# Narrow attention: maxima turned earlier, first head groups loaded in the projection, and an unread F32 product beside each early row pair

## The chip, the cores and the metric

The kernel runs on one core of a Trainium2 chip. The metric is device microseconds (us) of one execution. Before the change three runs gave 2531.52, 2533.64 and 2536.02 us; their median, 2533.64 us, is the time before. The engines are named as in the profile: PE is TensorE (PEld its weight loads), DVE VectorE, ACT ScalarE, POOL GpSimd, SP SyncE, which here only issues DMAs.

## The reference

The input `x` is 4 x 512 x 256 in F32. Four blocks follow one another, each `x = x + layernorm(block(layernorm(x)))`:

```
A  causal attention, 16 heads of 16: softmax(q k^T / 4, causal) v, then W_out + bias
B  mixture of 32 experts, 6 a token, squared relu, plus a shared expert
C  attention, 16 heads of 16 (q1|q2, k1|k2 of 8 each), no mask:
   softmax(q1 k1^T * s - lam * q2 k2^T * s) v, then W_proj
D  grouped attention (16 heads of 128, 4 key heads) and a mixture of 8 experts, 2 a token
```

The change touches stages A and C only: the projection that makes q, k and v, and the attention behind it.

## The kernel before

Stages A and C call the same three functions: `narrow_projection` (L160), `narrow_attention` (L590) and `narrow_output` (L954). Each is a block of its own with a barrier behind it.

The projection works through four groups of 512 tokens (one batch each). A group is normalized, transposed on PE, copied to `hT` by ACT, multiplied by the weights (8 products of 128x512 for q and k, 8 of 128x256 for v), and q and k are split into a high part in FP32R (ACT, L302) and a low part (DVE, L268). SP stores both parts to the DRAM tensors `q_parts` and `k_parts` with four DMAs of 512 KB (L209), waits until the group's stores have landed (L210) and only then lets ACT write the parts of the next group (`parts_free`, L211). POOL fills the spare rows of the attention's tiles `qs` and `ks` meanwhile: zeros for q, ones for k (L280, L281).

The attention works in quads of four heads: 4 quads a batch, 16 in a stage. A quad's q and k lie in SBUF as two slots of two heads; a head has rows 0 to 47 for three partial products of the high and low parts, and rows 48 and 49 of q for the negated row maximum (high and low), against ones in k. There are four buffers `qs[0..3]`, `ks[0..3]`. Loading a quad takes 12 DMAs of 64 KB (`load_half`, L648). For each quad PE makes the scores twice:

- `rows` (L692): scores with queries on the partitions, one pair of heads at a time, in two PSUM places; DVE takes the row maxima (L913), which frees the place. In stage A masks are added by four small products a pair (L706).
- POOL splits the maxima (L866, L868), `turn_maxima` (L723) transposes them on PE, `keep_maxima` on ACT copies them to `mT` (L812), and SP places them with four DMAs in the q tiles (`place_maxima`, L663).
- `cols` (L730): scores with keys on the partitions, now with the maximum subtracted by the extra rows; ACT takes exp (L829), POOL cuts the diagonal in stage A (L882), and `values` (L739) multiplies by v in F32 with a sum column; `turn_quad` (L752) and DVE divide.

PE's order is written out by hand: at the start the `rows` of quads 0 and 1 (L785 to L792), then in quad n, for each of the four key tiles kt, `cols` of the next tile, `rows` of quad n+2, the turn of the maxima of quad n+1 after kt = 1, the turn of quad n-1's output at kt = 2, and `values` of tile kt. Scores by key, the turned maxima and the turned output share a ring of three PSUM banks; `place`, `TM_AT` and `TQ_AT` give each its position in that ring. ACT follows the same order and copies the maxima after the exps of kt = 2.

The loads of quads 0 and 1 are issued when the attention block begins, q by SP and k by ACT; then SP issues the two loads of the mask in stage A (L674, L675) and quads 2 and 3.

Of the kernel before, what the change touches and what calls it, by code (L numbers as in the profile page):

```python
# [5 lines left out]
F32 = mybir.dt.float32  # L6
# [153 lines left out]
def narrow_projection(c, name, w_qk, w_v, b_qk, b_v, lambdas, q_parts, k_parts, qs, ks, vals):  # L160
# [5 lines left out]
    with ExitStack() as ctx:  # L166
# [18 lines left out]
        stored, parts_free, constant = sem("stored"), sem("parts_free"), sem("constant")  # L185
        tr, ps, pv = c.bank[0:2], c.bank[2:6], c.bank[6:8]
# [6 lines left out]
        with block:  # L193
            @block.sync
            def _(sp):
                sp.sem_inc(parts_free, 1)
                sp.dma_start(wqk[:, :, :], weights(w_qk)).then_inc(w_in, 16)
# [7 lines left out]
                with sp.Fori(0, B) as b:  # L205
# [5 lines left out]
                    sp.sem_inc(parts_free, 1)  # L211

# [377 lines left out]
def narrow_attention(c, name, q_parts, k_parts, qs, ks, vals, out, mask):  # L590
# [19 lines left out]
    with ExitStack() as ctx:  # L610
# [17 lines left out]
        loaded = [sem(f"loaded{s}") for s in range(4)]  # L628
# [18 lines left out]

        def load_half(eng, t, src, parts, quad, s):  # L648
            for g in range(2):
                for j, part in enumerate(parts):  # L650
                    r = PAIR * g + HD * j
                    rows = src[part, bass.ds(quad, 1), :, :].rearrange("a (u g d) s -> g d (a u) s", g=2, d=HD)[g]
                    eng.dma_start(t[r:r + HD, :, :].bitcast(F32), rows).then_inc(loaded[s], 16)

        block = nc.Block()
        with block:
            @block.sync
            def _(sp):
                def load_quad(quad, s):
                    load_half(sp, qs[s], q_parts, (0, 0, 1), quad, s)  # L660
                    load_half(sp, ks[s], k_parts, (0, 1, 0), quad, s)

                def place_maxima(n, s):  # L663
                    sp.wait_ge(mT_ready, n + 1)
                    for slot in range(2):
                        for g in range(2):
# [9 lines left out]
                for s in range(2, 4):  # L676
                    load_quad(s, s)
                place_maxima(0, 0)
                with sp.Fori(0, B - 1) as b:
                    for s in range(BQ):  # L680
# [3 lines left out]
                        load_quad(n + 4, s)  # L684
                for s in range(BQ - 1):
                    place_maxima(NQUAD - BQ + s + 1, s + 1)
                for s in range(4):
                    sp.wait_ge(m_loaded[s], 64 * B)

            @block.tensor  # L690
            def _(pe):
                def rows(n, s, qt, slot, first):  # L692
# [9 lines left out]
                    if causal:  # L702
                        for i in range(2):
                            for g in range(2):
# [3 lines left out]
                                if i == 1:  # L708
                                    mm.then_inc(rows_done, 1)

# [19 lines left out]
                def cols(b, s, kt, slot):  # L730

                    lo = first_query(kt)
                    if kt == 0 and slot == 0:
                        pe.wait_ge(m_loaded[s], 64 * b + 64)
# [23 lines left out]
                def quad(b, s, ahead, following, first):  # L758
# [3 lines left out]
                    for kt in range(NQ):  # L762
                        for slot in range(2):
# [1563 lines left out]
```

## Time and profile before

| what | value |
|---|---|
| runs, median | 2533.64 us |
| profiled execution | 2537.47 us |
| its span, first to last instruction | 2535.6 us |
| busy: PE, DVE, ACT, POOL | 79%, 66%, 48%, 29% |
| mean granted PE clock | 0.854 of 2.4 GHz |
| stage A: projection, attention, output | about 12 to 81, 81 to 371, 372 to 444 us |
| stage C: projection, attention, output | about 888 to 969, 969 to 1208, 1209 to 1242 us |

The page's slices of PE's clock (tenths, 63.4 us each) begin 9 5 5 5 5 5 6 6 9: the digits from the second to the sixth are the attention of stage A, where PE is granted about half its clock. The shares of busy time above are means over stages with different limits, so they say little of one stage; the rows further on are by stage.

### The profile page before, as it was taken

Reading aid. Unit: us, or ns where it says so; the run is one execution under the profiler, and the core shown is the slowest. Engines: PE = TensorE matmul, PEld = TensorE weight load, DVE = VectorE, ACT = ScalarE, POOL = GpSimd, SP = SyncE. Lnnn points to the kernel's source line nnn. Section 1 sums busy time; section 2 is a strip of 40 time slices with the busy share of each in tenths; the row PEclk is TensorE's granted clock in tenths of the full one; section 3 lists DMA queues with packets and bytes.
Section 4 is the critical chain, followed back from the end, with each engine's and each line's share of the span. In section 5 each row is a group of like instructions: output and inputs, shape, how many; then the busy total and the mean of one; then the engine's idle time right before and its main releaser. Section 6 shows DMA issues by size and latency. Waiting matters only on the chain. (4 is left out here: it accounts for less than half of the span.)

```text
span 2535.6 us, 41622 instructions
## 1 busy us (share of the span) xinstructions
PE 2010.2 (79%) x12514; PEld 1565.1 (62%) x12514; DVE 1670.2 (66%) x3522; ACT 1222.4 (48%) x2616; POOL 729.7 (29%) x817
## 2 busy tenths in 40 slices
PE   6599986399999765887477769999979807999990
PEld 3366645299999632332355537677759707999990
DVE  5344426788888775785678767777754416888865
ACT  1144431244444312777145448888863206777750
POOL 3022222255555430000145544444430140000005
PEclk9555556699999976999789889999989758999995
DMA  3511100000000025220122223222236316555523
GB/s 122 115 52 52 51 8 1 33 17 25 25 25 17 0 92 120 59 62 25 71 83 83 99 112 109 83 108 107 83 132 213 112 66 243 207 207 213 215 106 99
DMA packets 93281, 231.54 MB, mean 91 GB/s; under 512 B 13456, under 2 KB 39184, under 8 KB 86032
## 3 DMA queue, kind: packets, MB, share of 16 engines
q1 hardware_dynamic: 88976, 220.59, 25.2%
q0 software_dynamic: 3072, 8.39, 1.0%
q10 hardware_dynamic: 1152, 1.57, 0.5%
q8 instruction: 40, 0.66, 0.1%
q14 instruction: 41, 0.34, 0.0%
HBM read 157.10 MB, written 72.88 MB: 91 GB/s over the span
## 5 line engine op out<-in xcount | busy, mean ns | idle before, releaser
L544 POOL TENSOR_SCALAR d_att_probs<-d_att_probs,d_att_rinv 128x128 f32<-128x128 f32 (+2 forms) x192 | 177.6, 925 | 219.2 <-DVE d_att_rinv L555 219.1
L1439 DVE SCALAR_TENSOR_TENSOR b_acc<-bank,b_gates,b_acc 128x256 f32<-128x256 f32 x512 | 212.4, 477 | 41.7 <-PE bank L1354 41.7
L1407 POOL TENSOR_TENSOR b_moe_act_low<-b_moe_act,b_moe_act_high 128x512 fp32r<-128x512 f32 x136 | 175.9, 1294 | 177.5 <-ACT b_moe_act_high L1384 177.5
L434 PE MATMUL wide<-d_att_k,d_att_q 128*128 128x128 f32 (+3 forms) x512 | 188.1, 450 | 18.7 <-DMA d_att_k<-k_dram 18.5
L2017 PE MATMUL wide<-e_moe_hT_high,e_moe_w_high 128*128 128x256 f32 x644 | 183.2, 284 | 14.2 <-DVE e_moe_w_low L2087 14.2
L913 DVE TENSOR_REDUCE a_att_rmax<-wide 128x2 f32<-128x256 f32 (+3 forms) x128 | 104.7, 824 | 130.2 <-PE wide L706 129.6
L913 DVE TENSOR_REDUCE c_att_rmax<-wide 128x2 f32<-128x1024 f32 x128 | 155.3, 1223 | 49.9 <-PE wide L698 45.2
L2017 PE MATMUL wide<-e_moe_hT_high,e_moe_w_low 128*128 128x256 f32 x644 | 183.0, 284 | 0.0
L2017 PE MATMUL wide<-e_moe_hT_low,e_moe_w_high 128*128 128x256 f32 x644 | 183.0, 284 | 0.0
L491 ACT ACTIVATE d_att_probs<-wide,d_att_nmax 128x128 f32<-128x128 f32 (+3 forms) x256 | 135.4, 529 | 78.8 <-DVE d_att_nmax L550 78.8
L829 ACT ACTIVATE c_att_probs<-bank 128x512 f32<-128x512 f32 x256 | 139.1, 596 | 56.8 <-PE bank L736 52.3
L2087 DVE TENSOR_TENSOR e_moe_w_low<-e_moe_w,e_moe_w_high 128x768 fp32r<-128x768 f32 x161 | 151.3, 954 | 22.2 <-ACT e_moe_w_high L2047 19.7
L829 ACT ACTIVATE a_att_probs<-bank 128x512 f32<-128x512 f32 (+3 forms) x256 | 98.0, 435 | 127.3 <-PE bank L736 126.9
L1354 PE MATMUL bank<-b_moe_w_high,b_moe_act_high 128*128 128x256 f32 x544 | 153.4, 282 | 1.9 <-POOL b_moe_act_low L1407 1.9
L1354 PE MATMUL bank<-b_moe_w_high,b_moe_act_low 128*128 128x256 f32 x544 | 153.9, 283 | 0.0
L1354 PE MATMUL bank<-b_moe_w_low,b_moe_act_high 128*128 128x256 f32 x544 | 153.9, 283 | 0.0
L550 DVE TENSOR_REDUCE d_att_nmax<-wide 128x1 f32<-128x128 f32 (+3 forms) x256 | 124.9, 488 | 33.4 <-PE wide L436 33.3
L2150 POOL DMA_INDIRECT e_out_got<-y_slots,e_pos x32 | 31.3, 979 | 394.9 <-PEq L2144 385.7
L1343 PE MATMUL wide<-b_moe_h_high,b_moe_w_high 128*128 128x512 f32 x272 | 108.3, 398 | 41.1 <-DVE b_moe_h_low L1447 41.1
L1613 POOL TENSOR_TENSOR d_in_rot<-d_in_xc,d_in_xs 128x512 f32<-128x512 f32 x80 | 104.3, 1306 | 109.0 <-DVE d_in_xs L1578 109.0
L2047 ACT CAST e_moe_w_high<-e_moe_w 128x768 fp32r<-128x768 f32 x161 | 131.3, 833 | 8.0 <-DMA e_moe_w<-in_e_w 8.0
L1384 ACT CAST b_moe_act_high<-b_moe_act 128x512 fp32r<-128x512 f32 x136 | 84.3, 620 | 103.7 <-DVE b_moe_act L1424 103.7
(361 smaller groups left out, 6172.8 us busy)
## 6 DMA issues: line engine op xcount, KB each, us to landing
e_moe_w<-in_e_w SPq DMA_DIRECT2D x23, 2688.0 KB, 9.8
q_dram<-d_in_rot SPq DMA_DIRECT2D x16, 1024.0 KB, 3.9
d_att_q<-q_dram SPq DMA_DIRECT2D x16, 1024.0 KB, 4.9
o_dram<-d_att_o SPq DMA_DIRECT2D x64, 256.0 KB, 2.0
d_out_oT<-o_dram SPq DMA_DIRECT2D x16, 1024.0 KB, 5.6
b_moe_w<-in_b_w SPq DMA_DIRECT2D x17, 512.0 KB, 3.4
a_q<-q_parts SPq DMA_DIRECT2D x96, 64.0 KB, 2.2
c_q<-q_parts SPq DMA_DIRECT2D x96, 64.0 KB, 2.2
```

Source lines behind the costliest of these rows:

```text
L434: nc.tensor.matmul(stile[qt], qs[s][:, u, qt * P:(qt + 1) * P], ks[s][:, 0, 0:w], start=True, stop=False)
L491: nc.scalar.activation(probs[j % 2][:, qt, 0:width[qt]], stile[qt], ACT.Exp, bias=nmax[:, j, qt:qt + 1], accum_out=rsum[:, j, qt:qt + 1]). ...
L544: g.tensor_scalar(tile, tile, rinv[:, j, qt:qt + 1], None, ALU.mult).then_inc(scaled, 1)
L550: nc.vector.tensor_reduce(nmax[:, j, qt:qt + 1], stile[qt], AX.X, ALU.max, negate=True).then_inc(max_ready, 1)
L829: nc.scalar.activation(probs[kt % 2][:, hq, lo:S], cbank[place(kt, hq) % 3][:, lo:S], ACT.Exp).then_inc(exp_done, 1)
L913: nc.vector.tensor_reduce(rmax[s % 2][:, qt, 2 * slot:2 * slot + 2], rpair[slot][:, :, 0:keys(qt)], AX.X, ALU.max, negate=True).then_inc(m ...
L1354: mm = nc.tensor.matmul(py[2 * i + q // 2][:, (q % 2) * D:(q % 2 + 1) * D], ap[x][:, u % 4, q * P:(q + 1) * P], wp[s][y][:, i, WC:], start ...
L1407: g.tensor_tensor(ap[1][:, u % 4, :], act[:, u % 4, :], ap[0][:, u % 4, :], ALU.subtract).then_inc(act_low, 1)
L1439: nc.vector.scalar_tensor_tensor(out=tile, in0=y, scalar=gate, in1=tile, op0=ALU.mult, op1=ALU.add).then_inc(acc_done, 1)
L2017: mm = nc.tensor.matmul(ph[f % 4][:, i * SLOTS:(i + 1) * SLOTS], up[x][:, k, i, f * P:(f + 1) * P], hT[s][y][:, k, :], start=(n == 0), sto ...
L2047: nc.scalar.copy(wp[s][0][:, chunk[f]], ws[s][:, chunk[f]]).then_inc(w_high, 1)
L2087: nc.vector.tensor_tensor(wp[s][1][:, chunk[f]], ws[s][:, chunk[f]], wp[s][0][:, chunk[f]], ALU.subtract).then_inc(w_low, 1)
```

## The change

```diff
 # narrow_projection
-                with sp.Fori(0, B) as b:
+                sp.dma_start(raw_rows[:, :, :], ones).then_inc(ones_in, 16)     # ahead of the weights
+                sp.wait_ge(ones_ready, 1)
+                for b in range(B):
+                    sp.wait_ge(constant, 4 * b + 4)
+                    for g in range(2):
+                        r = P // 2 * g + 3 * HD
+                        sp.dma_start(ks[b][r:r + 4, :, :].bitcast(F32), one_rows[:, :, :].bitcast(F32)).then_inc(ones_put, 16)
                     for cc in range(4):
...
                     sp.wait_ge(stored, b * 64 + 64)
                     sp.sem_inc(parts_free, 1)
+                    if b < B - 1:
+                        load_quad(sp, qs[b], ks[b], q_parts, k_parts, b, loaded[b])
+                sp.wait_ge(ones_put, 16 * 2 * B)
...
-                        g.memset(ks[b][r:r + 32, :, :].bitcast(F32), 1.0).then_inc(constant, 1)
+                        g.memset(ks[b][r:r + 32, :, :].bitcast(F32), 0.0).then_inc(constant, 1)
...
+                a.wait_ge(ones_in, 16)
+                nc.scalar.copy(one_rows[:, :, :], raw_rows[:, :, :]).then_inc(ones_ready, 1)
 # narrow_attention
-        TM_AT, TQ_AT = 8, 13
+        TM_AT, TQ_AT = 4, 13
...
-            return r + (kt == 3) + 2 * (kt == 0)
+            return r + (kt in (2, 3)) + 2 * (kt == 0)
...
-                    for slot in range(2):
-                        for g in range(2):
-                            r, hq = PAIR * g + ROWS, 2 * slot + g
-                            sp.dma_start(qs[s][r:r + 2, slot, :].bitcast(F32), mT[s % 2][2 * hq:2 * hq + 2, :].bitcast(F32)
-                                         ).then_inc(m_loaded[s], 16)
-                load_half(sp, qs[0], q_parts, (0, 0, 1), 0, 0)
-                load_half(sp, qs[1], q_parts, (0, 0, 1), 1, 1)
+                    for g in range(2):
+                        r = PAIR * g + ROWS
+                        rows = mT[s % 2][4 * g:4 * g + 4, :].bitcast(F32).unsqueeze(1).to_broadcast([4, 2, S])
+                        sp.dma_start(qs[s][r:r + 4, :, :].bitcast(F32), rows).then_inc(m_loaded[s], 16)
...
-                for s in range(2, 4):
-                    load_quad(s, s)
+                load_quad(sp, qs[3], ks[3], q_parts, k_parts, 3, loaded[3])
...
+                def keep_busy():
+                    nc.tensor.matmul(obank[:, :], c.ident[:, :], c.x[:, 0:2, :].rearrange("p q d -> p (q d)"), start=True, stop=True)
...
+                        if kt == 1 and following:
+                            ring_free(n, TM_AT, first, True)
+                            turn_maxima(n + 1)
                         for slot in range(2):
...
-                        if kt == 1 and following:
-                            ring_free(n, TM_AT, first, True)
-                            turn_maxima(n + 1)
...
                             rows(s, s, qt, slot, s == 0)
+                            keep_busy()
...
-                        if kt == 2 and not (last and s == BQ - 1):
+                        if kt == 1 and not (last and s == BQ - 1):
...
-                load_half(a, ks[0], k_parts, (0, 1, 0), 0, 0)
-                load_half(a, ks[1], k_parts, (0, 1, 0), 1, 1)
```

Quads 0, 1 and 2 are now loaded by SP in the projection, each behind the stores of one token group; quad 3 at the start of the attention. The maxima are placed by two DMAs of four rows instead of four of two rows: both slots get the rows of both, and a pattern of ones and zeros in rows 48 to 51 of k picks the right ones (`one_rows`, two more DMAs a group in the projection); POOL writes the split maxima in the matching order. The turn of the maxima and ACT's copy of them come one key tile earlier. `keep_busy` multiplies the identity by 512 columns of `x` in F32 into the bank of the values; nothing reads it, and the first `values` overwrites it. It runs 8 times in quad 0's rows and 8 times in quad 1's, in each of the two stages.

## Rows read from the trace of the kernel before

**Rows 1.** Windows, A's attention: length, busy (count) PE PEld DVE ACT POOL, clock, DMA.
```profile
150.00:175.00 25.00, 23.90 (x152) 15.97 (x156) 10.03 (x15) 11.39 (x28) 6.65 (x19) 0.50 0.13 36
...
200.00:225.00 25.00, 22.54 (x180) 14.95 (x176) 11.66 (x17) 12.21 (x33) 7.64 (x21) 0.70 0.18 48
...
300.00:325.00 25.00, 22.43 (x180) 15.18 (x184) 12.25 (x17) 11.59 (x31) 6.00 (x16) 0.70 0.12 33
```

**Rows 2.** A window in stage C's attention, same columns.
```profile
1050.00:1075.00 25.00, 20.77 (x142) 7.59 (x135) 19.95 (x21) 18.46 (x35) 1.63 (x6) 1.00 0.24 65
```

**Rows 3.** Timeline at A's attention start: start us, us, engine, line, operation, idle before.
```profile
81.28 5.63 ACTq L653 DMA_DIRECT2D a_k<-k_parts  x12
...
86.80 0.42 SPq L674 DMA_DIRECT2D a_att_raw_pick<-in_a_pick  x1
...
97.53 0.48 PE L698 MATMUL wide<-a_k,a_q 48*128 48x128 f32 x2 [25.23 <-DVE a_att_never L939]
```

**Rows 4.** Timeline at C's attention start.
```profile
968.72 5.59 ACTq L653 DMA_DIRECT2D c_k<-k_parts  x12
...
977.18 1.22 PE L698 MATMUL wide<-c_k,c_q 48*128 48x512 f32 x4 [17.42 <-DMA c_k<-k_parts]
```

**Rows 5.** Timeline of one projection group in A.
```profile
56.46 2.18 ACT L302 CAST a_in_parts<-a_in_xp 128x512 fp32r<-128x512 f32 x4 [7.14 <-SPq L211]
...
60.59 1.07 ACT L295 COPY a_in_hT<-wide 128x512 f32<-128x512 f32 x2 [1.95 <-PE wide L318]
...
61.72 1.01 SPq L209 DMA_DIRECT2D q_parts<-a_in_parts  x2
```

**Rows 6.** F32 products 128x512 at the slow and at the fast clock (C's projection).
```profile
909.52 5.98 PE L326 MATMUL wide<-c_in_hT,c_in_wqk 128*128 128x512 f32 x7 [0.76 <-ACT c_in_hT L295]
...
940.44 3.60 PE L326 MATMUL bank<-c_in_hT,c_in_wqk 128*128 128x512 f32 x8
```

**Rows 7.** A row pair at the fast clock with masks (A), and DVE's two maxima of 512 keys.
```profile
211.48 0.43 PE L698 MATMUL wide<-a_k,a_q 48*128 48x512 f32 x2
...
211.71 0.34 PE L706 MATMUL wide<-a_att_never,a_att_pick 64*128 64x64 f32 x4
...
112.54 2.36 DVE L913 TENSOR_REDUCE a_att_rmax<-wide 128x2 f32<-128x1024 f32 x2 [0.32 <-PE wide L706]
```

**Rows 8.** Timeline, the first key-side scores of stage A.
```profile
113.84 0.79 PE L736 MATMUL bank<-a_q,a_k 64*128 64x512 f32 x2 [0.50 <-DMA a_q<-a_att_mT]
```

**Rows 9.** First key-side scores of C, its first three turns of maxima.
```profile
990.22 1.11 PE L726 MATMUL bank<-c_att_identr,c_att_mparts 128*128 128x128 f32 x4
...
995.57 0.79 PE L736 MATMUL bank<-c_q,c_k 64*128 64x512 f32 x2 [0.24 <-DMA c_q<-c_att_mT]
...
1005.53 0.66 PE L726 MATMUL bank<-c_att_identr,c_att_mparts 128*128 128x128 f32 x4
...
1018.64 0.66 PE L726 MATMUL bank<-c_att_identr,c_att_mparts 128*128 128x128 f32 x4
```

**Rows 10.** PE's waits in A from 125 to 350 us: total, times, longest.
```profile
PE bank L736 <- DMA a_q<-a_att_mT: 2.1, 2, 1.2
```

**Rows 11.** Timeline, turns of maxima in A around the first fast stretch.
```profile
206.03 0.66 PE L726 MATMUL bank<-a_att_identr,a_att_mparts 128*128 128x128 f32 x4
...
211.17 0.51 PE L736 MATMUL bank<-a_q,a_k 64*128 64x512 f32 x2 [1.19 <-DMA a_q<-a_att_mT]
...
219.72 1.11 PE L726 MATMUL bank<-a_att_identr,a_att_mparts 128*128 128x128 f32 x4
...
252.62 1.11 PE L726 MATMUL bank<-a_att_identr,a_att_mparts 128*128 128x128 f32 x4
```

**Rows 12.** Windows in A: the filling, inside the fast stretch, and its end.
```profile
115.00:120.00 5.00, 3.64 (x22) 2.61 (x26) 0.85 (x2) 3.62 (x8) 1.93 (x6) 0.50 0.00 0
...
209.00:212.00 3.00, 1.81 (x20) 1.12 (x18) 1.58 (x4) 0.28 (x1) 0.41 (x1) 1.00 0.18 51
...
215.00:216.00 1.00, 1.00 (x12) 0.92 (x16) 0.08 (x1) 0.82 (x3) 0.93 (x3) 0.64 0.64 162
```

More of the change, by code:

```diff
@@ L157, in _, with narrow_projection @@
                 g.memset(c.mhalf[:, :], -0.5)
-def narrow_projection(c, name, w_qk, w_v, b_qk, b_v, lambdas, q_parts, k_parts, qs, ks, vals):
+def narrow_projection(c, name, w_qk, w_v, b_qk, b_v, lambdas, q_parts, k_parts, qs, ks, ones, loaded, vals):
     nc = c.nc
@@ L587, in _, with narrow_attention @@
                     step(7, j, False, True)
-def narrow_attention(c, name, q_parts, k_parts, qs, ks, vals, out, mask):
+def narrow_attention(c, name, q_parts, k_parts, qs, ks, loaded, vals, out, mask):
     nc = c.nc
@@ L863, in split_maxima @@
                         g.wait_ge(max_turned, n)
-                    high, low = mparts[:, :, 0:8:2], mparts[:, :, 1:8:2]
+                    parts = mparts[:, :, 0:8].rearrange("p q (g s two) -> p q s g two", g=2, two=2)
+                    high, low = parts[:, :, :, :, 0], parts[:, :, :, :, 1]
+                    largest = rmax[i][:, :, :].rearrange("p q (s g) -> p q s g", g=2)
                     hold(g, spare)
-                    g.tensor_copy(high, rmax[i][:, :, :]).then_inc(split, 1)
+                    g.tensor_copy(high, largest).then_inc(split, 1)
                     g.wait_ge(split, 2 * n + 1)
-                    g.tensor_tensor(low, rmax[i][:, :, :], high, ALU.subtract).then_inc(split, 1)
+                    g.tensor_tensor(low, largest, high, ALU.subtract).then_inc(split, 1)
                 def hold_values(n, s, first):
@@ L2172, in _, with load_quad @@
                     add_normed(c, v, norm, b, lambda q: y[:, q, :], t, t_ready, x_ready)
+def load_quad(eng, q_t, k_t, q_parts, k_parts, quad, loaded):
+    for t, src, parts in ((q_t, q_parts, (0, 0, 1)), (k_t, k_parts, (0, 1, 0))):
+        for g in range(2):
+            for j, part in enumerate(parts):
+                r = P // 2 * g + HD * j
+                rows = src[part, bass.ds(quad, 1), :, :].rearrange("a (u g d) s -> g d (a u) s", g=2, d=HD)[g]
+                eng.dma_start(t[r:r + HD, :, :].bitcast(F32), rows).then_inc(loaded, 16)
 def build(nc, a, out):
@@ L2190, in build @@
             ks = [stage.enter_context(nc.sbuf_tensor(f"a_k{s}", [P, 2, S], F32R)) for s in range(4)]
-            narrow_projection(c, "a_in", a["a_wqk"], a["a_wv"], a["a_bqk"], a["a_bv"], None, q_parts, k_parts, qs, ks, vals)
-            narrow_attention(c, "a_att", q_parts, k_parts, qs, ks, vals, attended, {"pick": a["a_pick"], "never": a["a_never"]})
+            loaded = [c.sem(f"a_loaded{s}") for s in range(4)]
+            narrow_projection(c, "a_in", a["a_wqk"], a["a_wv"], a["a_bqk"], a["a_bv"], None, q_parts, k_parts, qs, ks, a["ones"], loaded, vals)
+            narrow_attention(c, "a_att", q_parts, k_parts, qs, ks, loaded, vals, attended, {"pick": a["a_pick"], "never": a["a_never"]})
             narrow_output(c, "a_out", attended, a["a_wout"], a["a_bout"], 1.0)
@@ L2213, in build @@
             ks = [stage.enter_context(nc.sbuf_tensor(f"c_k{s}", [P, 2, S], F32R)) for s in range(4)]
+            loaded = [c.sem(f"c_loaded{s}") for s in range(4)]
             lambdas = {"vectors": a["c_lambdas"], "halves": a["c_halves"]}
-            narrow_projection(c, "c_in", a["c_wqk"], a["c_wv"], None, None, lambdas, q_parts, k_parts, qs, ks, vals)
-            narrow_attention(c, "c_att", q_parts, k_parts, qs, ks, vals, attended, None)
+            narrow_projection(c, "c_in", a["c_wqk"], a["c_wv"], None, None, lambdas, q_parts, k_parts, qs, ks, a["ones"], loaded, vals)
+            narrow_attention(c, "c_att", q_parts, k_parts, qs, ks, loaded, vals, attended, None)
             narrow_output(c, "c_out", attended, a["c_wout"], None, 1.0 - LAMBDA_INIT)
@@ L2298, in laid_out @@
         "a_never": np.where(np.concatenate([never, never]), -1e38, 0.0).astype(np.float32),
+        "ones": np.repeat(np.kron(np.eye(2), np.ones((2, 1)))[:, :, None], S, axis=2).astype(np.float32),
         "before": (r[:, None] < r[None, :]).astype(np.float32),
```

22 lines of the change are left out of this document (7 added, 15 removed).

## Prediction

> **What bounds the kernel now.** I read the page's slices first (PE's clock is about half in the stretch 63 to 380 us, nearly full elsewhere), then windows of 25 us over both attentions, then timelines of one group or quad, and last the waits of PE. The numbers are of the profiled execution, 2537.5 us (span 2535.6 and 1.9 around it); the median of the runs is 3.8 lower.
>
> In stage A's attention PE is busy 23.9 of 25 us, at clock 0.50 [rows 1]: it is bound by PE at 1.2 GHz, and no wait ends last. Twice in the stage (the two windows with 0.70) the clock rises to 2.4 GHz for some 10 us and falls again. In C the same code without mask runs at 1.00, PE busy 20.8 of 25, DVE 20.0, ACT 18.5 [rows 2]: three engines share the bound, and extra PE work is not free there either. At both entries PE sits idle: 25.2 us in A, until the mask has come through the queue behind the loads, 17.4 us in C, until quad 0 has come [rows 3, 4].
>
> **The loads of quads 0 to 2 move into the projection.** A queue issues twelve 64 KB loads in 5.6 us [rows 3], so a quad costs SP 5.6 us, and the two new DMAs of ones 0.9 more. In a projection group the stores land at 56.46 (ACT's release), the next are issued at 61.72, 5.3 us later [rows 5]. With 6.5 us of new issues between them SP is the later one by 1.2 us, in each of the three groups behind a load, and each delay moves the next landing too: 3.6 us, and I add 0.3 a group for the load packets ahead of the stores: 4.5 us for each projection. PE does not see the first of these: ACT has the casts done at 58.64 and starts the next copy at 60.59, 1.95 us of slack; only the last group's stores come later. The source of the ones (a DMA of 0.4 us of issue and an ACT copy ahead of the first group) I cost at nothing, hidden by the first group's norm on DVE; without that cover it is 2 us a stage at most, about a DMA and a copy.
>
> At A's entry 24 loads no longer stand ahead of the mask. Before, the block began at 81.28, the mask was issued at 86.80 and rows began at 97.53, 16.3 us after the block. With the mask first: 0.85 us of issue, about 2.2 us to land, 0.5 us of DVE casts: 3.6 us. So 12.7 us gone less 4.5 us of projection: -8.2 in A. In C the 8.5 us from 968.72 to 977.18 become 0.2: -8.3 + 4.5 = -3.8. Together -12.0. Bounds: nothing is lost in the projection (-21), or the loads hold the stores by their full 5.5 us three times (+12).
>
> **The repeated product.** An F32 product of 512 columns is two instructions: 5.98/7 x 2 = 1.71 us at 1.2 GHz, 3.60/8 x 2 = 0.90 at most at 2.4, of which 0.86 when pipelined [rows 6]. There are 16 in a stage. A row pair of 512 keys takes PE 0.43 us when fast and 0.57 with A's masks, and DVE 1.18 us for its maxima [rows 7]; slow, a pair of 512 columns takes 0.79 [rows 8]. Before, the 16 pairs took 16.3 us in A (97.53 to 113.84) and 18.4 in C (977.18 to 995.57), there DVE's. Now a pair costs PE 2.4 to 2.5 us while slow and 1.32 (C) to 1.38 (A) while fast, above DVE's 1.18 either way, so cover by DVE is worth nothing once it has been filled. I expect two pairs slow, then the clock rises: during C's slow projection start it rose behind a few of just these products. A: 2 x 2.4 + 14 x 1.38 + 0.7 for the turn = 24.8, +8.5. C: 5 + 14 x 1.31 + 0.7 = 24.0, +5.6. Together +14.1; bounds: 16 fast and half hidden (+7), all slow (+47: 2.5 x 32 + 2.2 - 34.7).
>
> **C starts fast.** The first turn to the second is 15.3 us [rows 9], the second to the third 13.1, at the full clock; the first quad at that clock gives -2.2. Bounds: 0 and -3.
>
> **The maxima come sooner.** The turn, ACT's copy and the DMAs are the same work a key tile earlier, in the same ring with positions 4 to 8 exchanged; 2 DMAs instead of 4 take 1.0 us less to issue. The turn now waits for POOL's split a key tile sooner, and behind it on PE stand the next key-side scores, for which ACT waits. I take zero: at 1.2 GHz PE waited for the maxima 2.1 us in two waits from 125 to 350 us of A [rows 10], both in the fast stretches. Bounds: 0.3 us a quad either way (a changed order at ACT and PE), +-10. It matters only together with the clock: at 2.4 GHz the maxima are late by 1.19 us [rows 11], and this wait would go.
>
> **What the clock gives in A.** Slow, a quad takes (252.62 - 219.72)/2 = 16.45 us. From 206.03 to 219.72 one quad took 13.69, of which the clock was full until 215.28 (0.64 in the window from 215, [rows 12]) and then slow for 4.44. The part up to 215.28 is 12.01 us of slow work, done in 9.25, or 8.06 without the 1.19 of waiting [rows 11]. A quad all fast and without that wait is 16.45 x 0.67 = 11.0 us: 5.4 us less. Before, the two stretches gave 2.7 each.
>
> How many quads will be fast? The sixteen products raise the clock by the time key-side scores start. Then the pipeline fills: PE waits for exps, busy 3.64 of 5 us at the slow clock [rows 12], less at the fast one, and ahead of the falls in the steady state it was likewise thinly used (1.81 of 3 us in the same rows). So I give the raised clock an even chance to pass the filling. Behind it the thin part stays even without the wait for maxima: ACT's four exps of 512 at a quad's first key tile hold PE up in each quad. I expect the clock to fall within a few quads, to rise again two or three times as before, and each stretch to be longer than 10 us because the 1.19 us wait is gone. I take four quads' worth of fast clock: -21.6, against -5.4 that the kernel before had: -16.2. Bounds: none (+5.4) and 14 full quads (-70; the last two have less work).
>
> A rule of the Trainium skill reads this otherwise. By rows 1 PE is busy 24 of 25 us at 0.50. By "TensorE: Matmul & The Clock Gate", Part 1, a PE that is kept busy is let up to the full clock and stays there as long as no long idle stretch comes. By that rule A would have been fast before, which these rows contradict; but it also says that a clock once raised by the repeated products stays for the stage, and that is a rival below.
>
> **Sum.** -12.0 (loads) + 14.1 (products) - 2.2 (C's start) - 16.2 (A's clock) = -16.3: 2521.2 for the profiled execution, 2517.4 as a median; I say 2517.
>
> **Rivals.**
> 1. *The clock holds through stage A.* For it: C, the same loops, holds 1.00 for 200 us with PE busy only 20.8 of 25 [rows 2], and the wait that preceded both falls is removed. Against: A's products are narrower (128 to 512 columns, masks of 64), and ACT-bound thin stretches stay. 14 quads instead of 4: 54 us more, 2463. This is also what the skill's rule gives, by the same rows. Chance 0.16.
> 2. *The clock is given back at the filling and nothing is gained later.* The two short rises stay as they were; -12.0 + 14.1 - 2.2 = -0.1, 2533. For it: the filling's idle time [rows 12]; no product is repeated after it. Against: without the wait a later rise should last longer. Chance 0.21.
> 3. *Slower: SP's queue becomes the bound of the projections.* Place: between the stores' landing and the next stores, SP issues 14 DMAs, and their packets stand ahead of stores of 512 KB. The price is what each group's stores land later than my 1.5 us; at 4.0 us a group it is 2.5 x 6 = +15, with rival 2's clock 2548. On that clock the kernel is slower by over 5 us from 2.4 us a group on (5.6 / 6 more than my 1.5). For it: at A's entry the mask, issued at 86.80 behind loads from two queues, let PE start only at 97.53 [rows 3], so loads in the queue do hold up what follows. Against: there 24 loads stood ahead within 5.6 us from two issuers; here 12 from one, and the two ones DMAs pass before the stores. Chance 0.13.
> 4. *The products do not lift the clock.* Then they cost 47 instead of 14, and C's and A's gains go: -12 + 47 + 0 = +35, 2569. Against: the same F32 products lift it in both projections. Chance 0.05.
>
> My forecast, clock in parts, 2500 to 2530: 0.45.
>
> **How the numbers follow.** Single runs lay 4.5 us apart, so 0.2% (5 us, 2528.6 to 2538.7) is about what can be told from no change. Faster: 0.43 of the forecast's 0.45, rival 1's 0.16 and 0.05 of rival 2: 0.64. Same: 0.02 + 0.13 + 0.01 = 0.16. Slower: 0.03 + 0.12 + 0.05 = 0.20. The range reaches to rival 1 with ten fast quads or more and to rival 3: 2468 to 2546. It leaves out half of rival 1, a third of rival 3 and rival 4, about 0.2.
>
> **What would show it.** In the profile after: the projection of A ends 4 to 5 us later, rows start at about 89 and in C at 973 to 974; the sixteen pairs take 24 to 25 us in each stage; PE's clock is 1.00 before A's first key-side scores; in A's attention the clock share lies between 0.6 and 0.75 in place of about 0.53; no wait of PE for the maxima's DMA; C's quads at about 13.1 us or a little less, as before. A clock of 1.00 through A proves rival 1, one of 0.5 behind the filling rival 2, a projection longer by over 9 us rival 3. Stages B, D and the last one must not move by more than 3 us together; if they do, the sum is wrong in a place that I have not looked at.

## The result, and the profile after

The changed kernel takes 2551.38 us (2548.40 to 2554.20, 4 runs), the one before beside it 2534.39 (2531.52 to 2536.02, 4 runs): ratio 1.0061, 95% interval 1.0043 to 1.0079. It is slower: the medians lie 17 us apart, and the interval is 11 to 20 us (0.4 to 0.8%). Forecast was 2517; the range ended at 2546. A ratio leaves out executions over 1.5% above the fastest of their kernel; where a kernel of the experiments keeps its clock in some executions and loses it in others, its lowest and highest run are given too.

The profiled execution took 2552.12 us (span 2550.4), against 2537.5 before: +14.6. From stage marks of both traces:

```
part                                   before    after   change  forecast
A: start to first rows                   97.5     91.1     -6.4      -8.2
A: first rows to first key-side scores   16.3     28.7    +12.4      +8.5
A: those to the last attended           257.3    261.0     +3.7     -16.2
C: stage start to first rows             77.5     74.4     -3.1      -3.8
C: first rows to first key-side scores   18.4     29.8    +11.4      +5.6
C: those to the last attended           212.9    213.7     +0.8      -2.2
outputs of A, C; stages B, D, E             -        -     -4.3       0
```

The loads did nearly what was said. The pairs are the 16 early row pairs of a stage with their products, the filling is the stretch behind the first key-side scores, in which PE waits for the first exps. Of the 31 us between the forecast of the sum and the outcome, 20 are A's clock and 10 the pairs. Windows of the changed kernel (columns as in [rows 1]); the first three are A's row pairs, the filling and what follows, the next three answer to [rows 1], then C's pairs, C behind its filling, and the window of [rows 2]:

```profile
91.10:119.80 28.70, 28.70 (x132) 14.00 (x132) 12.86 (x16) 0.58 (x1) 0.78 (x3) 0.87 0.08 22
119.80:122.50 2.70, 1.17 (x7) 0.56 (x8) 0.33 (x1) 1.98 (x4) 0.42 (x1) 1.00 0.00 0
122.50:150.00 27.50, 26.58 (x172) 17.87 (x171) 10.47 (x14) 12.01 (x32) 7.57 (x21) 0.50 0.13 34
150.00:175.00 25.00, 23.90 (x158) 15.99 (x160) 11.53 (x17) 11.79 (x27) 6.04 (x17) 0.50 0.24 63
200.00:225.00 25.00, 24.66 (x164) 16.06 (x162) 12.06 (x17) 11.59 (x27) 6.42 (x19) 0.50 0.24 66
300.00:325.00 25.00, 23.78 (x166) 15.58 (x162) 10.57 (x15) 12.69 (x30) 6.41 (x18) 0.57 0.19 53
983.80:1013.60 29.80, 29.80 (x68) 9.85 (x68) 19.84 (x17) 0.57 (x1) 2.28 (x6) 0.79 0.10 28
1016.80:1027.10 10.30, 9.31 (x38) 3.39 (x36) 4.90 (x4) 4.81 (x10) 0.00 (x0) 0.50 0.02 3
1050.00:1075.00 25.00, 19.93 (x140) 7.31 (x136) 19.89 (x20) 18.52 (x36) 1.62 (x6) 1.00 0.25 67
```

The third number from the end is the clock. It is up when A's key-side scores start (119.8) and down at 122.5, after 2.7 us in which PE worked 1.17. Through the rest of A it is 0.50, as before, but for two short rises. In C the pairs are PE's (29.80 of 29.80 us) where DVE has 19.84 to do, and the clock falls behind that filling too, for 10.3 us.

The timeline of A's entry answers to [rows 3]: the mask is issued at the block's start, and rows begin 4.6 us behind it, 1.0 more than I had reckoned:

```profile
86.49 0.36 SPq L672 DMA_DIRECT2D a_att_raw_pick<-in_a_pick  x1
...
91.07 0.47 PE L695 MATMUL wide<-a_k,a_q 48*128 48x128 f32 x2 [19.08 <-DVE a_att_never L941]
...
93.85 0.47 PE L695 MATMUL wide<-a_k,a_q 48*128 48x128 f32 x2
...
94.63 2.07 PE L710 MATMUL bank<-x,ident 128*128 128x512 f32 x2
...
96.63 0.58 PE L695 MATMUL wide<-a_k,a_q 48*128 48x256 f32 x2
```

From pair to pair that is 2.78 us (93.85 to 96.63), of which the product takes 2.00 (from 94.63), not 1.71. The same timeline at the end of the pairs and in the filling, answering to [rows 7, 8]:

```profile
116.56 0.50 PE L695 MATMUL wide<-a_k,a_q 48*128 48x512 f32 x2
...
118.19 0.50 PE L695 MATMUL wide<-a_k,a_q 48*128 48x512 f32 x2
118.53 0.31 PE L703 MATMUL wide<-a_att_never,a_att_pick 64*128 64x64 f32 x4
118.77 1.12 PE L710 MATMUL bank<-x,ident 128*128 128x512 f32 x2
119.82 0.50 PE L737 MATMUL bank<-a_q,a_k 64*128 64x512 f32 x2
121.04 0.49 PE L737 MATMUL bank<-a_q,a_k 64*128 64x512 f32 x2 [0.72 <-ACT a_att_probs L831]
122.34 0.56 PE L737 MATMUL bank<-a_q,a_k 64*128 64x384 f32 x2 [0.81 <-ACT a_att_probs L831]
```

A fast pair takes 1.63 us, and the product in it 1.05 (118.77 to 119.82), against 1.38 and 0.86 in the forecast. Then two waits for ACT, 0.72 and 0.81 us, and the clock is gone; in C's filling the same two waits stand ahead of the fall at 1016.8. The wait for the maxima's DMA of [rows 10] is gone too; of PE's waits from 125 to 350 us the longest that names data is now ACT's:

```profile
PEld bank L737 <- ACT a_att_probs L831: 12.7, 43, 0.8
```

In the projection (timeline, answering to [rows 5]) SP issues twelve loads and the ones between the landing and the next stores, 6.8 us in place of 5.3; the projections end 5.2 and 5.4 us later (forecast 4.5):

```profile
57.66 2.68 SPq L2184 DMA_DIRECT2D a_q<-q_parts  x6
60.38 2.76 SPq L2184 DMA_DIRECT2D a_k<-k_parts  x6
63.18 1.23 SPq L213 DMA_DIRECT2D a_k<-a_in_one_rows  x2
64.46 0.95 SPq L217 DMA_DIRECT2D q_parts<-a_in_parts  x2
```

### The profile page after: what moved, and what is told of

Same layout as the page of the kernel before. It is cut to its first block and busy times, and to the rows that moved or that the text cites. A ratio compares the mean times of both kernels' runs of the same rounds, so it can differ in the third digit from the quotient of the medians.

```text
span 2550.4 us, 41604 instructions
## 1 busy us (share of the span) xinstructions
PE 2047.5 (80%) x12578; PEld 1574.1 (62%) x12578; DVE 1671.2 (66%) x3522; ACT 1225.9 (48%) x2618; POOL 732.6 (29%) x817
```

## The experiments

All ratios are to the kernel before, run beside each.

### Which part costs: three kernels

**no_products**: the changed kernel without `keep_busy()` beside the pairs.

```diff
                             rows(s, s, qt, slot, s == 0)
-                            keep_busy()
```

> The changed kernel without the 32 unread products; earlier maxima and moved loads stay. Theory (the products cost what their stretch grew by and give nothing back): the stretches from first rows to first columns shrink again from 28.7 to 16.3 us in A and from 29.8 to 18.4 us in C, so 23.8 us less than the changed kernel: 2527.6, and with A's further +3.7 us (columns to last attended) also gone, 2524; that is 7 to 10 us faster than the kernel before. Rival (the clock that they lift is worth part of what the prediction said, 16 us): 2535 to 2544. Rival (the moved loads cost too, the projection being 5.2 and 5.4 us longer): not below the kernel before's 2534.

2531.74 us (12 runs), ratio 0.9976 (0.9963 to 0.9989). So the products cost about 22 us (1.0061 against 0.9976), and the rest of the change is 3 to 9 us faster than before: the rival of 2535 to 2544 falls, and so does the one by which nothing is left of the gain. By the medians (2531.74 against 2536.80) it is 5 us, less than the 7 to 10 that the theory had. It is a little less than 25, the pairs' own difference, as this kernel's A has less full clock (below). Its row pairs, A and C:

```profile
90.20:105.80 15.60, 14.00 (x100) 12.71 (x100) 10.96 (x15) 0.57 (x1) 0.78 (x3) 0.50 0.16 42
...
972.40:990.30 17.90, 12.79 (x38) 5.50 (x38) 17.21 (x16) 0.57 (x1) 2.23 (x6) 0.50 0.17 47
```

In C they are bound by DVE (17.21 of 17.90) at PE's slow clock: no PE clock could have shortened them. In A PE has 14.00 and DVE 10.96 of 15.60, some room. The pairs are 13.1 and 11.9 us shorter than with products.

**products_alone**: the kernel before with that one call (and its function) and nothing else.

> The kernel before with the 32 products and nothing else of the change. Theory (products cost 24 us and the clock is given back at the filling of the pipeline): 2534 + 24 = 2558, at most 2562 with A's extra 3.7 us. Rival (products plus late loads or late maxima behave otherwise; the clock passes the filling where the maxima are turned late): 2534 + 14 - 16 = 2532.

2560.16 us, ratio 1.0079 (1.0048 to 1.0111): +23 beside its own before (2536.80), the theory's figure. Pairs: A 32.6 us, C 30.0; A's attention behind them 261.1.

**late_maxima**: no_products with the turn behind the rows of kt = 1 and ACT's copy at kt = 2, as before.

```diff
-        TM_AT, TQ_AT = 4, 13
+        TM_AT, TQ_AT = 8, 13
...
-            return r + (kt in (2, 3)) + 2 * (kt == 0)
+            return r + (kt == 3) + 2 * (kt == 0)
```

> The changed kernel without the products and with the maxima turned in their old place (ring position 8, after kt = 1's rows): what is left of the change are the loads in the projection, the row constants and the two broadcast transfers of the maxima. Theory (an earlier turn is worth nothing while TensorE is at 1.2 GHz, as it never waited for it long: rows 10): the same as without products and with early maxima, 2524 to 2528, within 3 us. Rival (the earlier turn costs or gains in A, where columns to last attended grew by 3.7 us, 0.26 us a quad): 2520 to 2522, or it is worth up to 10 us: 2534 to 2538.

2526.65 us (12 runs), ratio 0.9945 (0.9925 to 0.9965). The loads alone are worth 10 us by the medians (forecast 12.0); at the two entries the trace shows 7.3 and 3.6 us. By the medians the late turn is 5 us quicker than no_products' early one, more than the theory's 3; only the rival of 2520 to 2522 had that sign. The traces put it down to the clock's rises and not to the turn. In A's attention this kernel had 6.8 us of full clock in its profiled execution, no_products none, the changed one 9.5, the one before 20.5. A steady quad at 1.2 GHz takes 16.4 us with either turn, the two quads with a rise take 15.2 and 15.3, and A's attention is 2.4 us shorter, which is about these two. The runs without a trace point the same way (mean clock 0.851 to 0.861, no_products 0.848 to 0.852). Whether the late turn makes the rises likelier was not tried.

### What holds the clock: five kernels

**held**: the changed kernel with more unread work in A: while the pipeline fills, and ahead of the rows of kt = 3 and kt = 0 in every quad.

```diff
-                def rows(n, s, qt, slot, first):
+                def rows(n, s, qt, slot, first, wide=False):
...
+                    if causal and wide:
+                        nc.tensor.matmul(rpair[slot][:, 0, 0:P], c.ident[:, :], c.ident[:, :], start=True, stop=True)
...
+                def fill():
+                    nc.tensor.matmul(obank[:, 0:D], c.ident[:, :], c.x[:, 0, :], start=True, stop=True)
...
                 cols(0, 0, 0, 0)
+                if causal:
+                    fill()
                 pe.wait_ge(exp_done, 1)
                 cols(0, 0, 0, 1)
+                if causal:
+                    fill()
...
+                            if causal and first and kt == 0:
+                                fill()
                             if ahead:
...
-                                rows(n + 2, rs, kt, slot, False)
+                                rows(n + 2, rs, kt, slot, False, kt in (0, 3))
```

> The changed kernel with further unread work of TensorE in A alone, where it idled or where its products are thin: F32 128 x 256 products while the pipeline fills (2 ahead of quad 0, 2 in its kt = 0), and one F32 128 x 128 product ahead of each row pair at kt = 3 and kt = 0 (up to 4 a quad, 14 quads). Theory (the clock falls at the filling and in the thin stretches of a quad, and full array work holds it): A's attention stays at 2.4 GHz, its quads take 11 to 12 us in place of 16.4, 2551 - 14 x 4.5 = about 2488, between 2480 and 2505. Rival (it is not these stretches; the clock falls anyway): each extra product costs 0.43 us at 1.2 GHz, 56 x 0.43 + 4 x 0.9 = +28 us, 2575 to 2580.

2493.71 us, ratio 0.9840 (0.9815 to 0.9865), inside the theory's range. Windows of A: the filling, and behind it:

```profile
119.80:122.50 2.70, 2.44 (x11) 1.17 (x10) 0.29 (x1) 2.02 (x4) 0.42 (x1) 1.00 0.00 0
122.50:150.00 27.50, 26.19 (x248) 17.24 (x250) 14.12 (x20) 16.04 (x41) 9.50 (x27) 1.00 0.22 61
150.00:200.00 50.00, 47.78 (x458) 30.38 (x451) 28.71 (x41) 28.29 (x72) 16.62 (x45) 1.00 0.24 68
```

PE is busy 2.44 of the filling's 2.7 us in place of 1.17, the clock stays at 1.00 until 300 us, and A's key-side scores to last attended take 199.4 us in place of 261.0. A steady quad takes 12.1 us from turn to turn, in the changed kernel 16.4 at the slow clock:

```profile
187.61 0.66 PE L732 MATMUL bank<-a_att_identr,a_att_mparts 128*128 128x128 f32 x4
...
199.73 0.66 PE L732 MATMUL bank<-a_att_identr,a_att_mparts 128*128 128x128 f32 x4
```

**filling_only** has the `fill()` lines of that edit alone (`rows` called as in the changed kernel):

> The changed kernel with the four F32 128 x 256 products while A's pipeline fills, but none in the quads. Theory (the thin stretches of a quad let the clock fall by themselves): the clock passes the filling at 119.8 to 122.5 us and falls within the first two quads, by about 150 us; each fast quad is worth some 4.5 us: 2551 + 1 - 5 to 10 = 2542 to 2547. Rival (only the filling dropped it): A stays fast, 2551 - 63 = 2488, or less still, as no quad carries extra products.

2545.81 us, ratio 1.0031 (1.0009 to 1.0053), as the theory has it:

```profile
121.60:126.00 4.40, 4.13 (x22) 2.15 (x22) 0.52 (x2) 3.05 (x7) 1.67 (x6) 1.00 0.00 0
126.00:137.70 11.70, 9.93 (x112) 6.68 (x116) 6.69 (x9) 7.17 (x19) 4.01 (x12) 1.00 0.20 54
137.70:150.00 12.30, 11.99 (x73) 7.28 (x72) 4.46 (x8) 4.14 (x13) 2.28 (x6) 0.50 0.19 56
```

The clock passes the filling and falls at 137.7, in the second quad. **quads_only** has the other half, the products in `rows` without any `fill()`:

> The changed kernel with one F32 128 x 128 product ahead of each row pair of kt = 3 and kt = 0, and none while the pipeline fills. Theory (the clock falls at the filling, at 122.5 us as in the changed kernel; the quads' extra products are too few to lift it again): all quads at 1.2 GHz with 56 x 0.43 us more, 2551 + 24 = 2575. Rival (with them in place the clock rises again in the quads): between 2490 and 2530, by how soon it rises.

2578.39 us (2535.05 to 2605.78). The profiled execution, 2578.76 us:

```profile
120.30:123.10 2.80, 1.27 (x7) 0.57 (x6) 0.29 (x1) 2.11 (x4) 0.41 (x1) 1.00 0.00 0
...
150.00:200.00 50.00, 49.64 (x281) 30.86 (x281) 18.90 (x27) 17.29 (x45) 10.09 (x27) 0.50 0.17 46
```

It falls at the filling, and then PE busy 49.64 of 50 us does not bring it back; it rose only at 338 us (in the run of 2535 us presumably sooner; that one has no trace). A quad takes 20.0 us there, against 16.4 without its four products. To hold the clock in each run both stretches must be filled.

**held_late_maxima**: held with late_maxima's edit.

> The kernel 'held' (clock kept at 2.4 GHz through A's attention) with the maxima turned at their old, late place. Theory (rows 10: TensorE waited 2.1 us where it met full clock once; at 2.4 GHz a quad is 12.5 us and the maxima's way through ScalarE and the DMA no longer fits behind the rest): it waits 1 to 2 us in each of 14 quads, 10 to 25 us slower than held's 2494, that is 2504 to 2519. Rival (the turn's place doesn't matter at 2.4 GHz either, as C's attention took 212.9 and 213.7 us with late and early turn): within 3 us of held, 2491 to 2497.

Its runs lay between 2497.92 and 2574.06 us, their mean clock between 0.897 and 0.861; held's between 2492.42 and 2500.32. In the fastest, which is the profiled one, A's attention takes 204.4 us against held's 199.4, and PE waits again for the maxima:

```profile
PE bank L742 <- DMA a_q<-a_att_mT: 6.3, 14, 0.9
PEld bank L742 <- DMA a_q<-a_att_mT: 3.7, 4, 1.0
```

So at full clock the early turn is worth 5 us by one profile of each (a steady quad takes 12.4 to 12.6 us in place of 12.1), below the 10 I had expected at least. Beyond that it keeps the clock from being lost in some executions, by the mean clock of the runs; those have no trace. That is what the change's second part is good for, and only here.

**stacked**: the changed kernel with its 16 products of a stage in one row ahead of the first pair.

```diff
+                for i in range(16):
+                    keep_busy()
                 for s in range(2):
                     pe.wait_ge(loaded[s], 192)
...
                             rows(s, s, qt, slot, s == 0)
-                            keep_busy()
```

> The changed kernel with its 16 products of a stage ahead of the first row pair instead of one behind each pair. It tells the price of a product from its place. Theory (a product between row pairs costs more than in a stream, as its weights and the pair's are each loaded again; in C the pairs without products are bound by VectorE's maxima, 17.2 us busy of 17.9, so a product behind a pair only stretches it): the products themselves take some 4 x 1.75 + 12 x 0.87 = 17.4 us a stage; in A 4.6 us of it lie in the idle wait for the mask, so 12.8 there and 17.4 in C; with the rows behind them at 15.6 less some 2 (fast) and 17.9: A 28 to 29 us from mask to first columns, C 35 us. Total 2551 + 5 = 2556 (2551 to 2562). Rival (a product costs the same wherever it stands, and the rows at 2.4 GHz are then quicker): A 13 + 12, C 17 + 12, 2545 or less.

2563.24 us, ratio 1.0112 (1.0073 to 1.0151), above the forecast's 2562 by one. I had put them behind the wait for the mask, so none lay in that idle time. The timeline:

```profile
91.28 16.46 PE L710 MATMUL bank<-x,ident 128*128 128x512 f32 x32 [18.61 <-DVE a_att_never L942]
107.67 0.33 PE L695 MATMUL wide<-a_k,a_q 48*128 48x128 f32 x2
```

16.4 us for 16; the clock is slow until 96.3, and with three at 1.71 ([rows 6]) the other 13 took 0.87 each. In a stream the product has the forecast's price, beside a pair it costs 1.05. The pairs behind them, with nothing between, wait for DVE, and the clock falls among them, at 113.4 in A and 1007.7 in C; they take 14.2 and 17.6 us (no_products: 15.6 and 17.9).

### What it takes, and the cheapest version: seven kernels

**held_lean**: held, but three of the products ahead of A's wait for the mask, 256-column products in place of the 512-column ones, and none in C.

```diff
                 if causal:
+                    for i in range(3):
+                        keep_busy()
                     pe.wait_ge(mask_ready, 2)
...
                             rows(s, s, qt, slot, s == 0)
-                            keep_busy()
+                            if causal:
+                                fill()
```

> As held, but in A three F32 128 x 512 products ahead of the wait for the mask (TensorE idles 4.6 us there, 86.5 to 91.1) and 128 x 256 products in place of 128 x 512 ones behind the row pairs, and in C no products. Theory (products cost what their stretch grows by; the idle time is free; the clock is up from the first rows): C's stretch 29.8 to 17.9 us, -12; A's from 28.7 to 16 to 20 us, -9 to -13 (12.2 us of it are DVE's maxima and can't go): 2494 - 21 to -25, 2469 to 2473. Rival (with half-size products the clock doesn't rise before the quads, or falls at the filling): A at 1.2 GHz, 2540 to 2560.

2473.50 us, ratio 0.9758 (0.9737 to 0.9779), at the upper end of what was expected (2473). Row pairs of A, a stretch of its quads, its last two quads, the pairs of C:

```profile
90.80:109.30 18.50, 18.50 (x135) 12.55 (x134) 12.36 (x16) 0.58 (x1) 0.78 (x3) 1.00 0.11 30
...
150.00:200.00 50.00, 48.03 (x462) 30.99 (x462) 28.94 (x42) 29.46 (x76) 17.10 (x48) 1.00 0.27 71
...
285.00:311.00 26.00, 20.46 (x104) 8.28 (x96) 1.83 (x6) 10.63 (x29) 5.76 (x15) 0.50 0.01 3
914.10:932.10 18.00, 12.87 (x38) 5.60 (x38) 17.29 (x16) 0.57 (x1) 2.30 (x6) 0.50 0.17 46
```

The clock is 1.00 from the first pair on, bought in time in which PE idled.

**leaner**: held_lean with 128-column products beside A's pairs.

```diff
                             if causal:
-                                fill()
+                                nc.tensor.matmul(obank[:, 0:P], c.ident[:, :], c.ident[:, :], start=True, stop=True)
```

> held_lean with F32 128 x 128 products behind A's first row pairs in place of 128 x 256. Theory (from 90.8 to 109.3 us TensorE is busy all the time and VectorE's maxima 12.4 us, so TensorE bounds it; 16 products of 0.43 us become 16 of 0.33, in elapsed time 0.2 each less): 2 to 4 us less, 2470 to 2472, the clock still held. Rival (the work gets too thin and the clock falls at the filling): 2520 or more.

2474.93 to 2590.44 us over seven runs, four of them at 2562 or more. In the profiled one (2562.33) the clock rose at 91.9 and fell 3.4 us later, among the pairs. Nothing saved, and the hold lost: here is the lower end.

**half_quads**: held_lean with the quads' products at kt = 0 alone (`kt == 0` for `kt in (0, 3)`).

> held_lean with the quads' products only at kt = 0 (2 a quad in place of 4). Theory (TensorE is the bound of a quad at 2.4 GHz, busy 48.3 us of 50; each product of 0.33 us less is that much off; 28 of them): 2473 - 9 = 2464, if the clock holds. Rival (it takes both kt = 3 and kt = 0): the clock falls within some quads and the runs scatter between 2490 and 2540. The theory has no number for where this tips; 50 to 50.

2465.87 to 2548.34 us, median 2489.67. The best run is 7.6 us below held_lean's median, near the 9 that the theory promised; in the profiled one (2484.04) the clock was lost twice:

```profile
114.00:174.00 60.00, 54.42 (x550) 36.26 (x548) 35.05 (x49) 35.28 (x92) 20.42 (x58) 1.00 0.25 67
174.00:187.00 13.00, 12.97 (x78) 7.86 (x80) 4.67 (x8) 3.71 (x12) 2.93 (x8) 0.50 0.17 41
187.00:225.00 38.00, 35.52 (x358) 23.24 (x354) 23.63 (x32) 23.98 (x61) 13.15 (x36) 0.99 0.27 73
...
942.10:972.70 30.60, 28.02 (x108) 9.51 (x107) 15.29 (x14) 14.79 (x27) 0.84 (x3) 0.50 0.14 37
```

The two losses took back what the saved products gave: A's attention is 0.7 us longer than held_lean's. The other 11 us lie in C, as the last line shows: there, in code that is the same in both kernels, the clock rose 38.7 us behind the first key-side scores, in held_lean 8.1 us behind them:

```profile
940.20:970.90 30.70, 24.48 (x163) 9.05 (x163) 23.07 (x21) 22.70 (x43) 1.56 (x6) 1.00 0.21 55
```

C's attention takes 10.9 us more by it. So two executions can differ by 11 us through C alone, and differences of that size between these kernels need the trace of C beside them.

**thin**: held_lean with 32 columns of weights in the quads' products.

```diff
-nc.tensor.matmul(rpair[slot][:, 0, 0:P], c.ident[:, :], c.ident[:, :], ...)
+nc.tensor.matmul(rpair[slot][0:VW, 0, 0:P], c.ident[:, 0:VW], c.ident[:, :], ...)
```

> The kernel held_lean with the same number of products in the quads, of the same 128 columns, but 32 columns of weights wide (F32 128*32) instead of 128: a quarter of the array at work for the same time. It tells whether it is TensorE's busy time or how much of its array works that holds the clock. Theory (how much of the array works, since A's quads run at 0.50 with TensorE busy 96 to 99%, rows 1): the clock falls in the first quads, most of the 14 at 16.4 us or more: 2473 + 45 to 70 = 2518 to 2545. Rival (busy time): the same as held_lean, 2473, as the products take the same time.

2476.20 us, ratio 0.9765 (0.9727 to 0.9803): the clock holds, and my theory falls. The profiled execution (2480.25) has the late rise in C too, worth 10.8 us, and its A is 2.3 us shorter than held_lean's; a product takes 0.29 us in place of 0.33.

```profile
150.00:200.00 50.00, 47.88 (x470) 28.84 (x472) 29.49 (x43) 30.21 (x77) 17.42 (x49) 1.00 0.28 72
```

**few_rows**: the same with `c.ident[0:ROWS, :]` on both sides, 48 rows deep.

> held_lean with the quads' products 48 rows deep (F32 48*128, 128 columns) in place of 128. With 32 columns of weights (thin) the clock held: 2476.2. Theory A (TensorE's busy time alone holds it; what the product works on is nothing to the clock): 2473, as held_lean. Theory B (rows count, as A's own products of 48 and 64 rows leave it at 1.2 GHz with TensorE 96% busy, rows 1): the clock falls in the quads and runs scatter, 2500 to 2560.

2456.62 to 2484.72 us, median 2474.85, ratio 0.9732 (0.9680 to 0.9785). Neither theory: in the profiled execution (2482.49) the clock fell twice and came back by itself,

```profile
114.00:149.00 35.00, 31.21 (x339) 22.05 (x336) 20.92 (x29) 20.73 (x54) 11.56 (x32) 1.00 0.24 66
150.00:180.00 30.00, 29.79 (x188) 19.92 (x187) 11.69 (x17) 10.83 (x30) 6.27 (x17) 0.50 0.16 44
180.00:227.00 47.00, 43.53 (x480) 30.92 (x479) 30.13 (x42) 30.16 (x77) 16.86 (x46) 1.00 0.27 73
```

and the quads between are quicker than held_lean's, 11.1 to 11.2 us against 12.1. Four products of 0.27 us against 0.33 are 0.24 us of that; and ahead of held_lean's products the weight loads wait for their issue (7.1 us in 33 waits from 150 to 250 us), which few_rows' do not. The best run of all is one of these. Depth and time of the product changed together here, and what it is in the added work that holds the clock stays open.

**lean_both**: held_lean with the 256-column products and the filling in C too (`if causal` taken from each `fill()`).

> held_lean with the 128 x 256 products in C too: one behind each row pair and four while its pipeline fills. In C the pairs are bound by VectorE's maxima (1.22 us a pair, 17.2 of 17.9 us busy), so that a product of 0.43 to 0.5 us at 2.4 GHz hides. Theory (hidden once the clock is up; some 5 pairs before that at 1.2 GHz cost 0.7 us each; C is at 2.4 GHz 15 to 45 us sooner, worth up to 0.27 of that): -8 to +4, the median 2465 to 2477 and the runs closer together. Rival (they cost as the 512-column ones did, half of 11.4 us): 2478 to 2482.

2492.09 us, ratio 0.9819 (0.9802 to 0.9835): 18.6 us above held_lean by the medians, worse than both expectations.

```profile
915.00:945.70 30.70, 30.70 (x70) 13.64 (x70) 19.93 (x17) 0.57 (x1) 2.24 (x6) 0.50 0.10 27
...
950.00:972.00 22.00, 20.76 (x76) 7.07 (x74) 9.80 (x8) 9.85 (x18) 0.84 (x3) 0.50 0.14 37
```

The half-size products never lift C's clock (0.50 over all 30.7 us, PE busy all the time), so each costs its slow price: the pairs take 12.8 us more than held_lean's. The clock rose at 972.0, 26.3 us behind the first key-side scores, and C's attention takes 8.2 us more; as such late rises come without products in C too (half_quads, thin), this part can't be laid to the products for sure. In A the clock was up at the first pair, behind the three 512-column products, in every kernel that has these.

**lean_tail**: held_lean with the quads' products kept up in A's last two quads, which compute no rows.

```diff
                                 rows(n + 2, rs, kt, slot, False, kt in (0, 3))
+                            elif causal and kt in (0, 3):
+                                if kt == 0 and slot == 0:
+                                    pe.wait_ge(max_ready, 8 * NQUAD)
+                                nc.tensor.matmul(rpair[slot][:, 0, 0:P], c.ident[:, :], c.ident[:, :], start=True, stop=True)
```

> held_lean with the quads' products kept up in A's last two quads, which compute no rows and where the clock falls at 284.8 us, 26 us before the last output. Theory (26 us at 1.2 GHz hold some 20 us of work at 2.4, less eight products of 0.33 us): 3 to 6 us less, 2467 to 2471. Rival (with no rows to compute TensorE idles between the exponentials, so that the clock falls all the same): 2473 to 2476.

2472.95 us, ratio 0.9752 (0.9734 to 0.9770). From 285 to 308 us the clock is 0.93 in place of 0.50, and A's attention takes 197.0 us in place of 201.9 in the profiled executions; the medians differ by 0.6 us, within the spread of either. Inconclusive as a time. It and held_lean are the best versions that hold in each run: 2.4 to 2.5% below the kernel before.

## Why the prediction was wrong

- **Loads, -12.0: right in kind, 2.5 us less.** -6.4 and -3.1 at the entries, 9.5 together; late_maxima has 10 us by the medians. The mask's way took 4.6 us in place of 3.6, the groups 14.0 us in place of 12.3. Rival 3 (SP's queue, +15) did not come.
- **Products, +14.1: direction right, size wrong, +23.8.** Two terms of the sum: a product beside a pair costs 1.05 us at 2.4 GHz and 2.00 at 1.2, where I took the price of a stream (stacked: 0.87 and 1.71); and three pairs (A) to five (C) were slow where I took two. In the other kernels with these pairs the clock rose 8 to 16 us behind A's first rows and 5 to 13 behind C's, so this term moves by itself (A's pairs: 28.7 to 32.6 us). A: 3 x 2.8 + 13 x 1.5 + 0.8 is 28.7. C's bound was told rightly: DVE hides nothing of it, and without products its pairs are DVE's.
- **A's clock, -16.2: the step that failed.** "I give the raised clock an even chance to pass the filling" and "I take four quads' worth of fast clock". The clock was 1.00 ahead of the key-side scores, as said, and fell 2.7 us behind their start; with the later rises that made 9.5 us of full clock against 20.5 before: +3.7. There were two later rises, as I had said, but of 3.4 us each, where I had expected each to be longer than the 10 us of before once the 1.19 us wait was gone. Rival 2 described this, with 2533 (2537.4 for the profiled execution); 2537.4 + 9.7 (products' true price) + 2.5 (loads) + 3.7 (A) + 3.0 (C) - 4.3 (elsewhere) = 2552.0. My chance of 0.21 for it was too low: the row that I read for the filling (PE busy 3.64 of 5 us, at the slow clock) meant some half of that at the fast one, less than in the stretch ahead of the earlier falls. That an even chance at the filling should leave four quads as the likeliest was a mean over two cases, not a case.
- **What a fast quad is worth, 5.4 us: right.** held's steady quad takes 12.1 us, of which four added products of 0.33 us are 1.3; without them it would be some 10.8 (an estimate), against 16.4: 5.6 us less.
- **Why the wait's removal did not help.** The 1.19 us of [rows 11] are gone in the changed kernel, but the falls do not need them: the rise at 252.2 ended by 255.6 with PE waiting 0.64 us for ACT's exps. The early turn is worth 5 us and a steadier clock with the rest filled; nothing without, as the term of zero for it had said.
- **C's start, -2.2: +0.8.** The clock came early (996.3) but fell at C's filling too and was back at 1027.1; before, it rose once at 1003.8 and stayed.
- **The other stages:** D and E moved by 4.9 us together, more than the 3 I had allowed: D 742.7 to 739.8, E 530.8 to 528.8. Kernels that leave them alone show D at 742.7 (no_products), 741.9 (late_maxima) and 739.9 to 740.0 (held, products_alone, stacked). filling_only, with C as in the changed kernel, has 742.7. So both values come with the same C and D; what moves it was not tried.
- The Trainium skill ("TensorE: Matmul & The Clock Gate", Part 1) tells of a raised clock that is lost to long idle stretches between bursts of work, and of a second case in which short idle times that come often do it. The first does not match here: two waits of 0.72 and 0.81 us stood ahead of the fall. The second is nearer.

## What to carry to other kernels

Work added to lift a clock must reach to where the clock's gain is spent: look first for the thinnest stretch between the two, here the pipeline's filling and a few steps of each loop pass, and fill those. Before a small difference is read from two runs, compare the clock in the stages that the edit leaves alone, as a later rise in C alone made 11 us here. Price added work where it stands, not in a stream, and put it where the engine idles (three products ahead of a wait, with half-size ones behind, raised the clock sooner than sixteen full ones between pairs). Where another engine bounds the stretch, as DVE does C's pairs, a faster clock gives nothing there and the added work is paid in full.

## What the runs showed of the hardware

- Work that keeps the clock up need not raise it. At 1.2 GHz, a PE busy 49.64 of 50 us did not bring the clock up, with one 128-column F32 product ahead of each second pair or so (quads_only), nor did 30.7 us of pairs with 256-column F32 products (lean_both), while with pairs beside 512-column ones it rose after 7.5 us in A (91.1 to 98.6) and 12.5 in C (983.8 to 996.3), and after 5 to 16 us in the other kernels that have them. At 2.4 GHz, C's loops stay up with PE busy 19.93 of 25 us and A's fall (54.42 of 60, half_quads).
- To hold the clock, products of a quarter of the array's width did as well as full ones (2476 and 2474 us), against what I had held. Products 48 rows deep, which are also 0.06 us shorter, lost it twice in the one traced execution.
- Near the edge the same kernel's executions differ widely (leaner: 2475 to 2590 us, near 5%). Such a kernel needs more runs than three before it is judged.
